# Cross-attention in fp32 by split operands: the next batch's context tiles loaded and rounded earlier, their low parts split over two engines

## What is computed

```python
q = einsum('bcn,dc->bnd', x1, Wq) + bq          # d = 64
k = einsum('bcn,dc->bdn', x2, Wk) + bk[:, None]
v = einsum('bcn,dc->bdn', x2, Wv) + bv[:, None] # 512 channels
attn = softmax(einsum('bnd,bdm->bnm', q, k), axis=2)   # 1024 x 1024
out = einsum('bcm,bnm->bcn', v, attn) + x1
```

## Time and profile before

| what | value |
|---|---|
| median of 3 runs | 687.63 us (687.38 to 690.29) |
| span of the profiled execution | 687.4 us |
| PE busy | 656.8 us, 96% of the span |
| DVE busy | 475.1 us, 69% |
| ACT busy | 280.7 us, 41% |
| POOL busy | 139.3 us, 20% |
| DMA queue of SP | 99.91 MB, 51.1% of 16 engines |
| PE waiting for `pt_lo` of DVE | 17.5 us in 15 waits |

### The profile page before, as it was taken

One profiled execution on the slowest core, in us unless ns is written; L12 is line 12 of the kernel. 1 busy time (PEld: TensorE's weight loads), 2 busy tenths in 40 slices (PEclk: granted clock), 3 DMA queues, 4 the chain that ended last, 5 costly groups with the idle time before them and its releaser, 6 DMA issues.

```text
span 687.4 us, 8392 instructions
## 1 busy us (share of the span) xinstructions
PE 656.8 (96%) x2848; PEld 534.1 (78%) x2848; DVE 475.1 (69%) x503; ACT 280.7 (41%) x367; POOL 139.3 (20%) x58
## 2 busy tenths in 40 slices
PE   5999889999999989999899998999989999899997
PEld 3877668887788868888688886888868888788886
DVE  4889558695686765876758866679567695686641
ACT  5564422355235352354423633337232364234220
POOL 0302210063001440032400433005130063101200
PEclk9999989999999999999999999999999999999999
DMA  8400932749328482285624675255941749326351
GB/s 317 187 1 12 265 108 61 193 137 243 102 86 232 116 234 91 84 237 124 197 92 123 197 170 190 75 139 158 229 153 61 174 142 248 107 80 149 73 179 56
DMA packets 94874, 100.04 MB, mean 146 GB/s; under 512 B 8336, under 2 KB 69776, under 8 KB 94864
## 3 DMA queue, kind: packets, MB, share of 16 engines
q1 hardware_dynamic: 94864, 99.91, 51.1%
HBM read 51.64 MB, written 16.78 MB: 100 GB/s over the span
## 4 chain that ended last, share of the span: by engine, by line
PE 81%; DVE 6%; issue 4%; SPq 3%; ACT 3%; DMA 2%; DVEq 0%; ACTq 0%
PE acc_ps L731 39%; PE acc_ps L700 25%; PE s_ps L670 8%; PE s_ps L678 4%; PE s_ps L679 4%; DVE pt_lo L455 4%; SPq L208 3%; DMA stage<-in_ctx_dram 2%; ACT pt_hi L302 2%; ACT xs_hi L302 1%; DVE probs L497 1%; DVE blocks L506 1%; PE s_ps L794 1%; DVE negmax L490 1%; ACT probs L337 0%
## 5 line engine op out<-in xcount | busy, mean ns | idle before, releaser
L731 PE MATMUL acc_ps<-pt_hi,vt_hi 128*128 128x512 f32 x512 | 202.0, 395 | 17.5 <-DVE pt_lo L455 17.5
L731 PE MATMUL acc_ps<-pt_hi,vt_lo 128*128 128x512 f32 x512 | 200.5, 392 | 0.0
L731 PE MATMUL acc_ps<-pt_lo,vt_hi 128*128 128x512 f32 x512 | 200.4, 391 | 0.0
L731 PEld LDWEIGHTS acc_ps<-pt_hi,vt_hi 128*128 128x128 f32 x512 | 96.6, 189 | 44.0 <-DVE pt_lo L455 24.1
L337 ACT ACTIVATE probs<-s_ps,negmax 128x1024 f32<-128x1024 f32 x64 | 71.4, 1116 | 128.4 <-DVE negmax L490 128.4
L271 POOL TENSOR_TENSOR xs_lo<-stage,xs_hi 128x1024 fp32r<-128x1024 f32 x35 | 91.1, 2612 | 156.0 <-ACT xs_hi L302 156.0
L731 PEld LDWEIGHTS acc_ps<-pt_hi,vt_lo 128*128 128x128 f32 x512 | 96.7, 189 | 20.4
L731 PEld LDWEIGHTS acc_ps<-pt_lo,vt_hi 128*128 128x128 f32 x512 | 96.8, 189 | 19.8
L271 POOL TENSOR_TENSOR pt_lo<-pt_raw,pt_hi 128x1024 fp32r<-128x1024 f32 x14 | 41.0, 2946 | 327.5 <-ACT pt_hi L302 327.5
L700 PE MATMUL acc_ps<-wv_hi,xs_hi 128*128 128x512 f32 x256 | 99.9, 390 | 0.0
L700 PE MATMUL acc_ps<-wv_hi,xs_lo 128*128 128x512 f32 x256 | 99.7, 389 | 0.0
(11 more groups left out here) (49 smaller groups left out, 602.4 us busy)
## 6 DMA issues: line engine op xcount, KB each, us to landing
pt_raw<-blocks SPq DMA_DIRECT2D x240, 128.0 KB, 2.4
stage<-in_ctx_dram SPq DMA_DIRECT2D x32, 512.0 KB, 5.3
o_sb<-in_x_dram SPq DMA_DIRECT2D x64, 256.0 KB, 3.3
out_dram<-o_sb SPq DMA_DIRECT2D x64, 256.0 KB, 2.6
stage<-in_x_dram SPq DMA_DIRECT2D x28, 512.0 KB, 5.9
blocks<-in_x_dram SPq DMA_DIRECT2D x4, 512.0 KB, 8.6
pt_raw<-in_L_xattn_Wv_dram SPq DMA_DIRECT2D x4, 256.0 KB, 8.0
pt_raw<-in_L_xattn_Wk_dram SPq DMA_DIRECT2D x1, 128.0 KB, 3.4
```

The costliest lines, as they stand in the source:

```text
L731: mm = nc.tensor.matmul(acc_ps[:, c % BANKS, :], v[:, m, cols], p[:, m, :], start=(m == 0 and v is vt_hi and p is pt_hi), stop=(m == MT - ...
```

## The change

Three things are moved, and the semaphores are cut anew to fit. No operation is added or taken away.

- SP loads all four x2 tiles of the next batch between quadrants 1 and 2 of the moves, in the order 0, 2, 1, 3. Before, tile 0 stood there and the others behind the last quadrant.
- ACT rounds x2 tiles 2, 1, 3 right behind `q_high` and ahead of all four `p_hi`.
- The low parts of x2: POOL makes those of tiles 0 and 2. DVE makes that of tile 1 between `q_low` and `out(b, 0, 2)`, and that of tile 3 between `out(b, 0, 2)` and the four `p_lo`. The semaphores are one for the even tiles (POOL) and one for the odd (DVE).

```diff
@@ SP, batch @@
                 move(b, 1, range(0, 2))
                 if not last:
-                    next_x2(nb, 0)
+                    for k in (0, 2, 1, 3):
+                        next_x2(nb, k)
                 move(b, 1, range(2, NQ))
-                if not last:
-                    for k in range(1, KT):
-                        next_x2(nb, k)
                 store(b, 0, 0)
@@ POOL @@
-                for k in range(KT - 1):
-                    pool.wait_ge(s_x2hi, b * KT + KT + k + 1)
-                    low(xs_lo[:, k, :], stage[:, k, :], xs_hi[:, k, :]).then_inc(s_x2lo, 1)
+                for i, k in enumerate((0, 2)):
+                    pool.wait_ge(s_x2hi, b * KT + KT + i + 1)
+                    low(xs_lo[:, k, :], stage[:, k, :], xs_hi[:, k, :]).then_inc(s_x2lo_e, 1)
@@ ACT, batch @@
                     round_x2(nb, 0)
                     q_high(nb)
-                p_hi(b, 1, 0)
-                if not last:
+                    round_x2(nb, 2)
                     round_x2(nb, 1)
-                p_hi(b, 1, 1)
-                if not last:
-                    round_x2(nb, 2)
-                p_hi(b, 1, 2)
-                p_hi(b, 1, 3)
-                if not last:
                     round_x2(nb, 3)
+                for j in range(PAIRS):
+                    p_hi(b, 1, j)
@@ DVE @@
             def low_x2(b, k):
-                dve.wait_ge(s_x2hi, b * KT + k + 1)
-                return sub(xs_lo[:, k, :], stage[:, k, :], xs_hi[:, k, :])
+                dve.wait_ge(s_x2hi, b * KT + (1 if k == 0 else 4 if k == 3 else 3))
+                sub(xs_lo[:, k, :], stage[:, k, :], xs_hi[:, k, :]).then_inc((s_x2lo_e, s_x2lo_o)[k % 2], 1)
@@ DVE, batch @@
                     q_sum(nb)
                     q_low(nb)
+                    low_x2(nb, 1)
                 out(b, 0, 2)
-                for j in range(PAIRS - 1):
+                if not last:
+                    low_x2(nb, 3)
+                for j in range(PAIRS):
                     p_lo(b, 1, j)
-                p_lo(b, 1, PAIRS - 1)
-                if not last:
-                    low_x2(nb, KT - 1).then_inc(s_x2lo_last, 1)
                 out(b, 0, 3)
```

More of the change, by code:

```diff
@@ L135, in build @@
         s_x2hi = sem("s_x2hi")
-        s_x2lo = sem("s_x2lo")
-        s_x2lo_last = sem("s_x2lo_last")
+        s_x2lo_e = sem("s_x2lo_e")
+        s_x2lo_o = sem("s_x2lo_o")
         s_q = sem("s_q")
@@ L217, in batch @@
                 if not last:
-                    for k in range(KT - 1):
-                        sp.wait_ge(s_x2lo, b * (KT - 1) + k + 1)
+                    for k in range(KT):
+                        sp.wait_ge((s_x2lo_e, s_x2lo_o)[k % 2], b * 2 + k // 2 + 1)
                         load(x1_d, nb, k)
-                    sp.wait_ge(s_x2lo_last, b + 1)
-                    load(x1_d, nb, KT - 1)
                 move(b, 1, range(0, 2))
                 if not last:
-                    next_x2(nb, 0)
+                    for k in (0, 2, 1, 3):
+                        next_x2(nb, k)
                 move(b, 1, range(2, NQ))
-                if not last:
-                    for k in range(1, KT):
-                        next_x2(nb, k)
                 store(b, 0, 0)
@@ L601, in first_p_lo, with first_low_x2 @@
                 sub(pt_tile(pt_lo, t), turned(t), pt_tile(pt_hi, t)).then_inc((s_plo, s_plo_odd)[t % 2], 1)
+            def first_low_x2(k):
+                dve.wait_ge(s_x2hi, k + 1)
+                sub(xs_lo[:, k, :], stage[:, k, :], xs_hi[:, k, :]).then_inc((s_x2lo_e, s_x2lo_o)[k % 2], 1)
             nc.vector.memset(negmax[:], 0.0).then_inc(s_acc, BANKS)
             for k in range(KT):
-                low_x2(0, k).then_inc(s_x2lo if k < KT - 1 else s_x2lo_last, 1)
+                first_low_x2(k)
                 if k == 0:
@@ L748, in k_next @@
                 for k in range(KT):
[L749 to L752, removed]
+                    pe.wait_ge((s_x2lo_e, s_x2lo_o)[k % 2], b * 2 + k // 2 + 1)
                     mm = project_tile(wk_s, xs_hi, xs_lo, 1, k)
@@ L805, in _ @@
             for k in range(KT):
[L806 to L809, removed]
+                pe.wait_ge((s_x2lo_e, s_x2lo_o)[k % 2], k // 2 + 1)
                 mk = project_tile(wk_s, xs_hi, xs_lo, 1, k)
```

## The result

The changed kernel is slower by a little, 0.6%: 692.29 us (median of 20 runs) against 687.9 us for the kernel before (20 runs), a ratio of 1.0058 with a 95% interval of 1.0044 to 1.0072. The profiled execution has a span of 691.4 us, 4.0 more than the 687.4 of before. Of the 20 runs of the changed kernel, the eight with a granted clock of 0.987 or 0.988, the profiled one (693.22 us) among them, took 692.3 to 694.49 us, and the twelve with 0.990 or 0.992 took 688.5 to 693.07. The forecast was 682.9.

The account below looks back on a forecast made before the run. The prediction took PE's waits on `pt_lo`, 23.8 us, as the bound. Gains of 4.35 (five usual passes) and 1.8 (third), less 1.4 (first), cut the 687.4 us span by 4.75 to 682.65, median 682.9; range 677.5 to 689.

Parts of the forecast that it names:

- What bounds the kernel, and what is removed: PE's waits on `pt_lo`, 23.8 us in all, come from POOL's x2 subtractions beside `p_lo`; the change takes POOL out.
- The mechanism of the cost: Second half's front: `p_hi` 0 waits for moves until 334.1, `p_lo` 0 ends at 336.9, PE waits once, about 1.5 us.
- wait of 6.2 us: First pass: moves land at 85.2, `p_lo` 0 is ready at 87.55, and PE, free at 81.39, stands 6.2 us.
- the price of a load ahead of the moves: SP's DMA queue: each of three added loads delays the last move by 1.45 us, 4.35 in all.
- the 0.1 for the slower first matmul: Second half of a usual pass: PE's first matmul after a wait takes 0.34 instead of 0.226 us, charged as 0.1.
- the prediction's formula, 3L - 3.15: Loss in us of a pass other than the first, at L us a load, once L is above 1.58.
- The rival with the slower loads: Loads ahead of the moves take longer: gain gone at 1.79 us a load, 692 us at 2.0; chance 12%.
- My two ends: Two prices of an x2 load: 1.30 us from 404 GB/s, and 1.63 us from two loads landing in 3.26.
- The second failed step: the clock: PE's clock falls to 1.2 GHz behind the first pass's idle, between 0 and 3.2 us, taken as 3.2.

Follow-up runs that it names:

- e3_dve_behind: The kernel before, with POOL making only x2 tile 0's low part and DVE those of tiles 1, 2, 3 behind its four `p_lo`: 667.88 us.
- e8_all_behind: Against the kernel before: all x2 loads behind the moves, roundings behind `p_hi`, all low parts on DVE behind `p_lo`, none on POOL: 663.64 us.
- e4_dve_behind_loads4: The kernel of e3_dve_behind with all four x2 loads, instead of one, between quadrants 1 and 2 of the moves: 694.22 us.
- e7_after_wait_loads: The changed kernel, with SP also waiting until the last x2 load has landed before issuing quadrants 2 and 3 of the moves: 707.98 us.

## Why the prediction was wrong

**What bounds the kernel, and what is removed: right for passes 2 to 7.** PE's waits there were on POOL's collisions, and they are gone. e3_dve_behind takes away the collisions alone: 19.8 us by the balance, and 19.7 in the time. In the first pass they were worth only 3.5 of the 8.1 us, with the fall of the clock behind them. The other 4.6 stay in e3_dve_behind, and in e8_all_behind only 0.2 is left; they come at least in part from ACT's rounding of a tile whose load landed late. The prediction had counted every wait as a collision.

**The mechanism of the cost: right.** `p_hi` 0 waits for the moves, PE waits once a pass at step 0, the four `p_lo` take 1.16 us each, and POOL takes its turn between `q_low` and the low part of tile 1: POOL's second subtraction ends at 332.42, and DVE's, which takes 3.31 us, 1.08 behind it at 333.50. So DVE is through at 335.3 where 335.7 was forecast. The first pass had its wait of 6.2 us exactly as forecast, and its moves landed at 85.2, as forecast, because there each added load made the last move only 1.5 us later.

**The failed step: the price of a load ahead of the moves.** I took 1.45 us, in the middle between 1.30 and 1.63. In pass 4 the last move came 5.7 us later for three loads (335.45 with 0.06 of shift between the two clocks, against 329.77): 1.9 each. Over passes 2 to 7 the last move landed 14.1 us after the issue of the first load on average, against 8.8 before, which makes 1.76 us a load (1.5 to 2.0 by pass). e4_dve_behind_loads4 beside e3_dve_behind gives 1.69. So a load cost 0.3 us more than I took. Besides, I had counted from a single pass: in pass 4 of the kernel before the last move landed 8.4 us after that issue, the earliest of the six passes, which hid another 0.4 us a pass.

Together, PE's distance across the wait exceeds its own by 2.57 us on average over passes 2 to 7 (1.66 to 3.19), where 1.54 was forecast. With the 0.1 for the slower first matmul that is 2.67, which the prediction's formula, 3L - 3.15, gives at L = 1.94; this L holds both errors. The rival with the slower loads had this mechanism and its threshold right (no gain from L = 1.79, slower by over 0.5% from 1.95), but got 12%.

Why a load cost more is only partly shown. My two ends were both prices of a load with no move behind it, and e7_after_wait_loads shows that moves behind matter: with them the loads land 2.1 us apart, without them 1.5. But as moves land between the loads, most of these 0.6 us don't reach the last move: 1.76 is only 0.2 above the 1.54 of the loads alone. Why the price goes from 1.5 to 2.0 us from pass to pass stays open.

**The second failed step: the clock.** I priced its fall in the first pass only, at 3.2 us. There it cost about 1.5, because the granted clock was 0.50 from 84.0 us on, and PE stood until 87.67. But it fell in passes 2, 5 and 7 too and cost 1.6 us each time. PE's idle before these falls was 2.50, 3.03 and 2.45 us, and in passes 4 and 6, without a fall, 2.37 and 2.60. I had counted a wait at its own length. With two waits of 0.33 and 1.67 us (1.25 and 1.67 in pass 3) the kernel before didn't lose the clock in passes 2 to 7 of its profiled execution, so the change also traded two short idles for one long one. The three falls are those of the profiled execution; at a granted clock of 0.988 it is among the eight runs of 20 with the lowest, so others may have had fewer, which no trace shows.

**The sum in place of mine.** Six passes at 2.67 us instead of 1.6 are 6.4 us more, three falls of the clock 4.8, and the first pass 1.7 less than forecast (7.8 instead of 9.5): 682.65 + 6.4 + 4.8 - 1.7 = 692.15, against a span of 691.4. The 0.7 us between them are about what the balance, too, shows above the spans.

**The range** ended at 689.0, between no gain and the slower rival. It should have reached to 692, since nothing in the trace excluded a load of 2 us: single distances of 1.8 to 2.5 us between two loads were there to be read in passes 2, 4 and 5, and I had taken a middle instead of reading them all.

## What to carry to other kernels

A transfer moved ahead of another one in the same queue is paid by the one that has a deadline: ask which of the two has slack, and put the one with slack behind, even if the work that follows it then runs later. Price the transfer by the landing of the one that has the deadline, over all passes and not over one, and ask how long a single idle of TensorE becomes, not only what the idles sum to. And when two engines collide on one resource, look first whether the engine on the path has room for the other's work behind its own: here that gave 3% by itself (e3_dve_behind), and 3.7% with loads and roundings put behind as well (e8_all_behind).

## What the runs showed of the hardware

- A load of 512 KB with moves of 512-byte pieces queued behind it landed 2.1 us after its predecessor (18 distances in the changed kernel), and 1.5 us without them (18 in e7_after_wait_loads). The last load of a group went from 2.0 to 2.7 us down to 1.2 to 1.3. The last move, behind three more loads, came 1.76 us later for each of them.
- The granted clock fell to 0.50 behind single idles of 2.45, 2.50 and 3.03 us in the changed kernel and held behind 2.37 and 2.60. In e4_dve_behind_loads4 it fell in pass 5 behind an idle of 1.79 us and held in pass 6 behind 2.31. The length of the idle alone doesn't decide. Where PE had work again by the time of the fall, it cost 1.6 us in the changed kernel.
